# Beginning of a four-stage kernel: tokens loaded in two transfers, the second half's and the context's turns moved among the steps of the first norm

## The chip, the cores and the metric

The kernel runs on one core of one Trainium2 chip. The metric is the device time of one execution in microseconds (us). The median of three runs of the kernel before is 998.36 us (997.34 to 1002.92).

## The reference, cut to what matters

The program runs 1024 tokens (4 batches of 256) of width 256 through eight sublayers, each of the form `x = x + f(layernorm(x))`: expert FFN by token id, ternary FFN, WKV scan, mixture of experts, quantised attention, quantised FFN, linear attention, block-scaled FFN. The change touches only the first:

```
def _layernorm(x, axis=-1, eps=1e-05):
    m = jnp.mean(x, axis=axis, keepdims=True)
    v = jnp.var(x, axis=axis, keepdims=True)
    return (x - m) / jnp.sqrt(v + eps)
x = x + _L0_xattn_ref(_layernorm(x, axis=-1), itok_BxS_13_99985, ctx_2048, ctx_2048, ctx_2048)
...
for e in range(E):      # the expert's three weights are slices of ctx_2048
    g = jax.nn.silu(jnp.einsum('bsd,fd->bsf', hidden_states, Wg[e]))
    u = jnp.einsum('bsd,fd->bsf', hidden_states, Wu[e])
    y = jnp.einsum('bsf,df->bsd', g * u, Wd[e])
    out = jnp.where((expert_ids == e)[..., None], y, out)
```

So before the first product the kernel needs the tokens and the context with the feature dimension on the partitions, and the norm of the tokens.

## The kernel before, in words

Every engine has its own instruction list, written out by hand and executed in order; semaphores join them. The activations live transposed: `x_t` is 128 partitions x 2 feature blocks (KC) x 1024 tokens, and most work goes by halves of 512 tokens (TH = 2, HALF = 512). Half 0 is batches 0 and 1, half 1 is batches 2 and 3. The context is transposed likewise into `ctx_t`.

Loading. SyncE (SP) issues all DMAs of the beginning on one queue: tokens into `x_nat` (L648, semaphore load["x"]), context into `ctx_nat` (L649, load["ctx"]), token ids broadcast to all partitions (L650), and then the weights of several stages (helper `rows_in`, L656 and L658). Each DMA adds 16 to its semaphore when it has landed.

Turning. TensorE (PE) transposes 128x128 blocks with `pe.transpose` (L475, helper `pe_turn`). `tokens_turned` makes four groups for each of the two tensors, in the order (half 0, block 0), (half 0, block 1), (half 1, block 0), (half 1, block 1). So x has groups 0 to 3 and ctx groups 4 to 7. A group is four turns into one PSUM bank, 6 or 7 in alternation, and a copy out of it: even groups by ScalarE (ACT, L489), odd ones by VectorE (DVE, L487). A group may start when the group two before it has been copied out. `part_of(name, (i, n))` picks part i of n of the groups of a name; `evacuated` makes PE wait for a name's last two copies.

The norm "l0x" of half 0 is a chain over three engines: mean (`ln_mean_of`: four matmuls with `mean_w`, PE), centring (`ln_xc_of`, L2070, DVE), squares (`ln_sq_of`, L1667, ACT), sums of squares (`ln_var_of`: 16 matmuls with one column each, PE), square root (`ln_sd_of`, L1672, ACT, with another activation table), reciprocal and diagonal matrix (`ln_diag_of`, L2076 and L2080, DVE), rows (`ln_rows_of`: two matmuls, PE), product (`ln_xn_of`, L2086, DVE). The helper line of all these matmuls is L962. The mean waits for `x_ready`, which DVE raises after the copies. Half 1's norm is computed inside the expert stage, which follows as `ffn(l0x)`; DVE first makes the masks of the token ids for it (L2240 to L2244) and then gates (L2248, L2249). ACT's function there is Silu (L1702), in a third table.

In the kernel before, PE turns all of x, then computes the mean, turns all of ctx, and then does the sums and the rows.

Of the kernel before, what the change touches and what calls it, by code (L numbers as in the profile page):

```python
# [14 lines left out]
ACT = mybir.ActivationFunctionType  # L15
# [9 lines left out]
P = 128  # L25
D = 256
KC = D // P
BATCH = 4
SEQ = 256
TOK = BATCH * SEQ  # L30
TT = TOK // P
# [32 lines left out]
def build(nc, a, out, stop=None):  # L64
# [5 lines left out]
    with ExitStack() as ctx:  # L70
        def sb(name, shape, dt=F32):
            return ctx.enter_context(nc.sbuf_tensor(name, shape, dt))

        def sem(name):
            return ctx.enter_context(nc.semaphore(name))
# [3 lines left out]
        x_t = sb("x_t", [P, KC, TOK])  # L79
# [3 lines left out]
        sd = sb("sd", [P, TH, 4])  # L83
        rsd = sb("rsd", [P, TH, 4])
        rsd_diag = sb("rsd_diag", [P, 4, P])
        ctx_t = sb("ctx_t", [P, KC, TOK])
        act_buf = sb("act_buf", [P, 2, HALF])
        hid_buf = sb("hid_buf", [P, 2, HALF])
        ident = sb("ident", [P, P])
# [51 lines left out]
        c = Cut(0)  # L141
        ctx_nat = c([TT, D])
        x_nat = c([TT, D])
# [3 lines left out]
        c = Cut(c.at / 256)  # L147
# [6 lines left out]
        c = Cut(0)  # L154
# [4 lines left out]
        c = Cut(0)  # L159
# [4 lines left out]
        c = Cut(ARENA - 24 - 18)  # L164
# [5 lines left out]
        c = Cut(75.5)  # L170
# [26 lines left out]
        c = Cut(45.0625)  # L197

        slots = []
        for _ in range(2):  # L200
# [4 lines left out]
                d=c([KC, PACK + P]), dqa=c([PACK + P]), qb=c([P]), qb_rest=c([P]),  # L205
# [4 lines left out]
        def part_weights(b):  # L210
# [7 lines left out]
        c = Cut(0)  # L218
# [3 lines left out]
        c = Cut(0)  # L222
# [14 lines left out]
        c = Cut(0)  # L237
# [7 lines left out]
        c = Cut(92)  # L245
# [30 lines left out]
        c = Cut(0)  # L276
# [17 lines left out]
        c = Cut(c3.at / 256)  # L294
        wt_l3 = [c([KC, H3]), c([KC, H3]), c([8, D])]
        assert c.at / 256 <= late_at
        c = Cut(0)
# [13 lines left out]
        load = {n: sem("load_" + n) for n in ("ctx", "x", "tid", "l0", "l1", "mu", "moe0", "moe1",  # L311
                                               "l2w", "l2x", "l2", "l3x", "l3", "rows", "gate0", "gate1")}
        turned, evac_act, evac_dve = sem("turned"), sem("evac_act"), sem("evac_dve")
        weights_fixed = sem("weights_fixed")
        x_ready = sem("x_ready")
# [82 lines left out]
        def mark(name, f):  # L398
            first = len(groups)
            f()  # L400
            marks[name] = (first, len(groups))
# [12 lines left out]
        def tokens_turned(nat, dst, wait):  # L414
            for h in range(TH):
                for k in range(KC):
                    turns = [(P, P, j * P, nat[:, 4 * h + j, k * P:(k + 1) * P]) for j in range(4)]
                    groups.append((turns, [(dst[:, k, h * HALF:(h + 1) * HALF].unsqueeze(1), P, 0, 512, 512)],
                                   wait, 0))

        mark("x", lambda: tokens_turned(x_nat, x_t, (load["x"], 16)))
        mark("ctx", lambda: tokens_turned(ctx_nat, ctx_t, (load["ctx"], 16)))

        def three(ws, wts, h, wait, fixed):
            turn_in(h, ws[0], wts[0], wait, fixed)
# [39 lines left out]
        def pe_turn(pe, name, part=None):  # L465
            for g in part_of(name, part):
                turns, _, wait, fixed = groups[g]
                if g >= 2:
                    pe.wait_ge(*copied(g - 2))
                if wait:  # L470
                    pe.wait_ge(*wait)
                if fixed:
                    pe.wait_ge(weights_fixed, fixed)
                for m, w, col, src in turns:
                    last = pe.transpose(ps[0:m, 6 + g % 2, col:col + w], src, ident[0:src.shape[0], 0:src.shape[0]])  # L475
                last.then_inc(turned, 1)

        def copy_out(eng, name, dve, part=None):
            for g in part_of(name, part):
                if by_dve[g] != dve:  # L480
                    continue
                eng.wait_ge(turned, g + 1)
                for dst, m, col, step, n in groups[g][1]:
                    k = dst.shape[1]
                    src = ps[0:m, 6 + g % 2, col:col + k * step].rearrange("p (k n) -> p k n", k=k)[:, :, 0:n]
                    if dve:
                        last = eng.tensor_copy(dst, src)  # L487
                    else:
                        last = eng.activation(dst, src, ACT.Copy)  # L489
                last.then_inc(evac_dve if dve else evac_act, 1)  # L490
# [9 lines left out]
        def ffn_lag(s):  # L500
# [3 lines left out]
        l0x = dict(name="l0x", n=4 * KC, rows=[P] * 4 * KC,  # L504
                   w1=lambda k, i: ctx_t[:, k, i * P:(i + 1) * P], w3=None,
                   w2=lambda i, o: ctx_t[:, i % KC, (i // KC) * SEQ + o * P:(i // KC) * SEQ + (o + 1) * P])
# [138 lines left out]

        @block.sync
        def _(sp):
            sp.dma_start(x_nat, a["x"].rearrange("b (c p) d -> p (b c) d", p=P)).then_inc(load["x"], 16)  # L648
            sp.dma_start(ctx_nat, a["ctx_2048"].rearrange("b (c p) d -> p (b c) d", p=P)).then_inc(load["ctx"], 16)  # L649
            sp.dma_start(tid, a["itok_BxS_13_99985"].rearrange("b s -> (b s)").partition_broadcast(P)  # L650
                         ).then_inc(load["tid"], 16)
# [308 lines left out]
        def _(pe):  # L960
# [18 lines left out]
            def ln_var_of(name, h):  # L979

                n = 2 * LN[name] + h
                pe.wait_ge(ln_sq, n + 1)
                if n:

                    pe.wait_ge(xn_ready, n)
                for j in range(4):
                    for k in range(KC):
                        last = mm(ps[:, ln_row_bank(name, h), j:j + 1],
                                  ln_sq_tile(name, h)[:, k, j * P:(j + 1) * P], mean_w[:, 0:1],
                                  k == 0, k == KC - 1)  # L990
                last.then_inc(ln_var, 1)

            def ln_rows_of(name, h):

                pe.wait_ge(ln_diag, 2 * LN[name] + h + 1)
                mm(ps[:, ln_row_bank(name, h), :], ones[:, :], rsd_diag[:, :, :].rearrange("p a b -> p (a b)"), True,
                   True).then_inc(ln_rows, 1)
# [73 lines left out]
                return go  # L1071

            pe.wait_ge(const_ready, 1)
            pe_turn(pe, "x")
            ln_mean_of("l0x", 0)
            pe_turn(pe, "ctx")
            ln_var_of("l0x", 0)
            ln_rows_of("l0x", 0)
            evacuated(pe, marks["ctx"][1])

# [579 lines left out]
        def _(act):  # L1660
# [8 lines left out]
            def ln_sd_of(name, h):  # L1669
                n = 2 * LN[name] + h  # L1670
                act.wait_ge(ln_var, n + 1)
                act.activation(sd[:, h, :], ps[:, ln_row_bank(name, h), 0:4], ACT.Sqrt, bias=eps_col[:, :]  # L1672
                               ).then_inc(ln_sd, 1)
# [41 lines left out]
                    hidden_high(s, TH - 1, s["n"] - 1)  # L1715

            act.wait_ge(const_ready, 1)
            copy_out(act, "x", False)
            ln_sq_of("l0x", 0)
            copy_out(act, "ctx", False)  # L1720
            ln_sd_of("l0x", 0)
            def ternary_copied(name, wts, h, i):

                full, src, dst = h // P, ternary_back[name][i], wts[i]
                act.wait_ge(load[name], 16 * 8)
                if i == 2:
                    act.activation(dst.rearrange("p c (k j) -> p c k j", j=P),
                                   src.rearrange("p (k c j) -> p c k j", k=KC, j=P), ACT.Copy).then_inc(weights_fixed, 1)
                else:
                    v = src.rearrange("p (r k j) -> p k r j", k=KC, j=P)  # L1730
                    act.activation(dst[:, :, 0:full * P].rearrange("p k (r j) -> p k r j", j=P), v[:, :, 0:full], ACT.Copy)
                    act.activation(dst[:, :, full * P:], v[:, :, full, 0:h % P], ACT.Copy)
# [319 lines left out]
        def _(dve):  # L2052
# [14 lines left out]
            def ln_xc_of(name, h):  # L2067
                dve.wait_ge(ln_mean, 2 * LN[name] + h + 1)
                b = ln_bank(name, h)
                TTN(xc[:, h], x_t[:, :, tok(h)], ps[:, b:b + 1, :].to_broadcast([P, KC, HALF]), ALU.subtract  # L2070
                    ).then_inc(ln_xc, 1)

            def ln_diag_of(name, h):
                n = 2 * LN[name] + h
                dve.wait_ge(ln_sd, n + 1)
                step(dve.reciprocal(rsd[:, h, :], sd[:, h, :]))  # L2076
                if n:

                    dve.wait_ge(ln_rows, n)
                TTN(rsd_diag[:, :, :], ident[:, :].unsqueeze(1).to_broadcast([P, 4, P]),  # L2080
                    rsd[:, h, :].unsqueeze(2).to_broadcast([P, 4, P]), ALU.mult).then_inc(ln_diag, 1)

            def ln_xn_of(name, h):
                dve.wait_ge(ln_rows, 2 * LN[name] + h + 1)
                b = ln_row_bank(name, h)
                TTN(xn_t[:, :, tok(h)], xc[:, h], ps[:, b:b + 1, :].to_broadcast([P, KC, HALF]), ALU.mult  # L2086
                    ).then_inc(xn_ready, 1)
# [138 lines left out]
                step(last)  # L2226
                return TTN(v, v, b3(scale, MX_BLOCK), ALU.mult)

            copy_out(dve, "x", True)
            dve.wait_ge(evac_act, 2)  # L2230
            dve.wait_ge(evac_dve, 2)
            dve.sem_inc(x_ready, 2)
            ln_xc_of("l0x", 0)
            copy_out(dve, "ctx", True)
            ln_diag_of("l0x", 0)
            ln_xn_of("l0x", 0)

            dve.wait_ge(load["tid"], 16)
# [606 lines left out]
```

## Time and profile before

| | |
|---|---|
| median of three runs | 998.36 us (997.34, 998.36, 1002.92) |
| profiled execution, time | 1001.22 us |
| its span | 999.5 us |
| its mean granted TensorE clock | 0.91 of full |
| PE busy | 854.2 us, 85% of the span |
| DVE / ACT / POOL busy | 716.6 / 452.1 / 164.8 us |
| chain that ended last | PE 54%, DVE 26%, ACT 9% |

The profile is one execution; its engines are PE (matmul), PEld (weight load of the same engine, overlapping), DVE, ACT, POOL and SP's DMA queue. The span begins with the first instruction, and all times are microseconds from there. The time of the execution is 1.7 us longer than its span.

### The profile page before, as it was taken

Reading aid. Unit: us, or ns where it says so; the run is one execution under the profiler, and the core shown is the slowest. Engines: PE = TensorE matmul, PEld = TensorE weight load, DVE = VectorE, ACT = ScalarE, POOL = GpSimd, SP = SyncE. Lnnn points to the kernel's source line nnn. Section 1 sums busy time; section 2 is a strip of 40 time slices with the busy share of each in tenths; the row PEclk is TensorE's granted clock in tenths of the full one; section 3 lists DMA queues with packets and bytes.
Section 4 is the critical chain, followed back from the end, with each engine's and each line's share of the span. In section 5 each row is a group of like instructions: output and inputs, shape, how many; then the busy total and the mean of one; then the engine's idle time right before and its main releaser. Section 6 shows DMA issues by size and latency. Waiting matters only on the chain.

```text
span 999.5 us, 12145 instructions
## 1 busy us (share of the span) xinstructions
PE 854.2 (85%) x4470; PEld 521.9 (52%) x4470; DVE 716.6 (72%) x962; ACT 452.1 (45%) x695; POOL 164.8 (16%) x251
## 2 busy tenths in 40 slices
PE   5989984489889999999899787777778989889898
PEld 3434652244645555555455444445454758755566
DVE  1676669964557888778669889899894544459677
ACT  2214546642334322222123489899894545522111
POOL 1000000000004523334400063111110000002312
PEclk9899995579979999999999979898799999879899
DMA  8602003100132222141021899998781000000000
GB/s 256 216 0 48 1 0 57 13 3 7 17 51 41 36 29 34 44 66 17 3 45 31 156 172 168 165 164 141 143 136 39 21 0 1 1 1 1 10 11 22
DMA packets 211614, 59.17 MB, mean 59 GB/s; under 512 B 192398, under 2 KB 209892, under 8 KB 211556
## 3 DMA queue, kind: packets, MB, share of 16 engines
q1 hardware_dynamic: 211508, 58.30, 30.4%
q8 instruction: 36, 0.59, 0.2%
q10 hardware_dynamic: 48, 0.10, 0.1%
q14 instruction: 22, 0.18, 0.1%
HBM read 20.62 MB, written 1.05 MB: 22 GB/s over the span
## 4 chain that ended last, share of the span: by engine, by line
PE 54%; DVE 26%; ACT 9%; issue 8%; DMA 1%; POOL 1%; SPq 0%; DVEq 0%; ACTq 0%; POOLq 0%
PE ps L962 50%; ACT xc L1935 2%; DVE arena L2651 2%; PE ps L1412 1%; ACT sq L1935 1%; DVE arena L2285 1%; PE ps L475 1%; DVE arena L2660 1%; DVE arena L2215 1%; DVE xc L2457 1%; PE ps L1093 1%; DVE sq L2564 1%; ACT arena_split L1850 1%; DVE sq L2561 1%; DVE xc L2070 1%
## 5 line engine op out<-in xcount | busy, mean ns | idle before, releaser
L962 PE MATMUL ps<-arena 128*128 128x16 f16 (+8 forms) x1776 | 248.9, 296 | 47.3 <-ACT xc L1935 22.4
L962 PE MATMUL ps<-arena_split 128*128 128x512 f32 (+6 forms) x736 | 195.9, 429 | 17.2 <-DVE arena_split L2107 5.9
L962 PEld LDWEIGHTS ps<-arena 128*128 128x128 f16 (+4 forms) x1776 | 136.1, 125 | 122.3 <-issue 67.0
L962 PEld LDWEIGHTS ps<-arena_split 128*128 128x128 f32 (+6 forms) x736 | 131.7, 192 | 88.1 <-issue 39.7
L2651 DVE TENSOR_REDUCE arena<-ps 128x1 f32<-128x1024 f32 x128 | 151.5, 1220 | 14.8 <-PE ps L962 13.6
L1935 ACT ACTIVATE xc<-ps,arena 128x1024 int16<-128x1024 f32 x86 | 103.0, 1208 | 12.0 <-POOL arena L919 11.5
L962 PE MATMUL ps<-sq,arena 128*64 128x256 f32 (+3 forms) x256 | 78.7, 504 | 8.1 <-DVE sq L2564 8.0
L868 POOL TENSOR_SCALAR arena<-arena 128x512 f32<-128x512 f32 x12 | 23.1, 1922 | 245.3 <-DVE arena L2479 245.3
L919 POOL TENSOR_SCALAR arena<-arena 128x1 f32<-128x1 f32 x128 | 33.9, 265 | 177.5 <-DVE arena L2651 177.2
L1702 ACT ACTIVATE act_buf<-ps 128x512 f32<-128x512 f32 (+2 forms) x34 | 20.3, 596 | 85.5 <-PE ps L962 85.4
L1935 ACT ACTIVATE sq<-ps,arena 128x1024 int16<-128x1024 f32 x42 | 50.4, 1210 | 3.7 <-POOL arena L919 3.5
L962 PEld LDWEIGHTS ps<-sq,arena 128*64 128x64 f32 (+3 forms) x256 | 29.2, 161 | 42.2 <-issue 29.8
L962 PE MATMUL ps<-arena,ident_b 128*128 128x256 bf16 x224 | 49.3, 307 | 0.0
L962 PE MATMUL ps<-mean_w,sq 128*128 128x1 f32 x240 | 32.9, 267 | 18.5 <-ACT sq L1667 18.5
L936 POOL TENSOR_TENSOR arena<-arena 128x1024 f32<-128x1024 f32 (+1 forms) x9 | 17.5, 1948 | 184.2 <-DVE arena L2223 184.1
L962 PEld LDWEIGHTS ps<-mean_w,sq 128*128 128x128 f32 x240 | 32.7, 216 | 26.7 <-ACT sq L1667 24.7
L962 PE MATMUL ps<-x_t,mean_w 128*128 128x512 f32 x64 | 37.9, 723 | 7.9 <-DVE x_t L2307 4.4
L962 PE MATMUL ps<-xn_t,arena 128*128 128x256 f32 (+2 forms) x112 | 38.4, 489 | 0.0
L1850 ACT ACTIVATE arena_split<-xc 128x1024 fp32r<-128x1024 f32 x16 | 16.9, 1059 | 40.3 <-DVE xc L2457 40.3
L475 PE MATMUL ps<-ident,arena 128*128 128x128 f32 (+4 forms) x122 | 22.8, 342 | 14.1 <-DMA arena<-in_x 7.1
L2395 DVE TENSOR_TENSOR hid_buf<-ps,act_buf 128x512 f32<-128x512 f32 (+2 forms) x18 | 12.4, 690 | 30.5 <-ACT act_buf L1702 30.2
L962 PE MATMUL ps<-xn_t,ctx_t 128*128 128x512 f32 x64 | 33.0, 645 | 1.4 <-DVE xn_t L2086 1.4
(300 smaller groups left out, 1342.6 us busy)
## 6 DMA issues: line engine op xcount, KB each, us to landing
arena<-in_L_ffn_w SPq DMA_DIRECT2D x4, 640.0 KB, 6.1
arena_split<-arena_split SPq DMA_DIRECT2D x61, 32.0 KB
arena<-in_x SPq DMA_DIRECT2D x1, 1024.0 KB, 6.2
arena<-in_ctx SPq DMA_DIRECT2D x1, 1024.0 KB, 8.6
arena<-in_L_xattn_Wkv SPq DMA_DIRECT2D x2, 512.0 KB, 4.0
arena<-in_L_ffn_gate_w SPq DMA_DIRECT2D x1, 1024.0 KB, 10.1
arena<-in_L_ffn_up_w SPq DMA_DIRECT2D x1, 1024.0 KB, 12.6
arena<-in_L_ffn_down_w SPq DMA_DIRECT2D x1, 1024.0 KB, 12.6
```

What stands on the lines that cost most here:

```text
L475: last = pe.transpose(ps[0:m, 6 + g % 2, col:col + w], src, ident[0:src.shape[0], 0:src.shape[0]])
L868: step(pool.tensor_scalar(qf, qf, 2.0 ** -6, 1.5 * 2.0 ** 20, ALU.max, ALU.mult))
L919: pool.tensor_scalar(A["bias"][:, b:b + 1], A["nm"][:, b:b + 1], A["sq"][:, t, i:i + 1], math.log(255.0), ALU.mult, ALU.add).then_inc(att_ ...
L936: return pool.tensor_tensor(v, v, scale.unsqueeze(2).to_broadcast([P, n, MX_BLOCK]), ALU.mult)
L962: return pe.matmul(o, l, r, start=start, stop=stop)
L1093: return pe.transpose(ps[0:m, bank, col:col + n], src, ident[0:n, 0:n])
L1412: last = pe.transpose(ps[:, 7, :].bitcast(BF16)[:, k * P:(k + 1) * P], y[:, k * P:(k + 1) * P], ident_b[:, :])
L1702: act.activation(act_buf[0:r, u % 2, :], ps[0:r, 2 * (u % 2), :], func, scale=1.0 if scale is None else scale[0:r, :]).then_inc(act_ready, 1)
L1850: act.activation(moe["xe_parts"][:, n % 2, 0], moe["xe"], ACT.Copy).then_inc(moe_xh, 1)
L1935: act.activation(probs(u).rearrange("p (a b) -> p a b", a=2), ps[:, score_banks(u), :], ACT.Exp, bias=att_small["bias"][:, u % 3:u % 3 + 1 ...
L2395: return TTN(hid, up, s, ALU.mult)
L2651: dve.tensor_reduce(A["nm"][:, b:b + 1], ps[:, score_banks(u), :], AX.XY, ALU.max, negate=True).then_inc(att_max, 1)
```

## The change

The tokens come in two transfers of half the size; the second adds to load["ctx"], so that the value 32 means that the second half and the context are there, and 16 on load["x"] that the first half is. PE turns the first half, computes its mean, turns the second half and the first half of the context, does the sums, turns the context's second half, and does the rows. ACT and DVE place their copies accordingly. DVE raises `x_ready` once for each half. ACT begins with a copy of 128x4 elements into `sd`, which is overwritten later.

```
--- before.py
+++ after.py
@@ -416,10 +416,10 @@
                 for k in range(KC):
                     turns = [(P, P, j * P, nat[:, 4 * h + j, k * P:(k + 1) * P]) for j in range(4)]
                     groups.append((turns, [(dst[:, k, h * HALF:(h + 1) * HALF].unsqueeze(1), P, 0, 512, 512)],
-                                   wait, 0))
-
-        mark("x", lambda: tokens_turned(x_nat, x_t, (load["x"], 16)))
-        mark("ctx", lambda: tokens_turned(ctx_nat, ctx_t, (load["ctx"], 16)))
+                                   wait[h], 0))
+
+        mark("x", lambda: tokens_turned(x_nat, x_t, ((load["x"], 16), (load["ctx"], 32))))
+        mark("ctx", lambda: tokens_turned(ctx_nat, ctx_t, ((load["ctx"], 32), (load["ctx"], 32))))
 
         def three(ws, wts, h, wait, fixed):
             turn_in(h, ws[0], wts[0], wait, fixed)
@@ -645,7 +645,10 @@
 
         @block.sync
         def _(sp):
-            sp.dma_start(x_nat, a["x"].rearrange("b (c p) d -> p (b c) d", p=P)).then_inc(load["x"], 16)
+            sp.dma_start(x_nat[:, 0:TT // 2, :], a["x"][0:BATCH // 2].rearrange("b (c p) d -> p (b c) d", p=P)
+                         ).then_inc(load["x"], 16)
+            sp.dma_start(x_nat[:, TT // 2:TT, :], a["x"][BATCH // 2:BATCH].rearrange("b (c p) d -> p (b c) d", p=P)
+                         ).then_inc(load["ctx"], 16)
             sp.dma_start(ctx_nat, a["ctx_2048"].rearrange("b (c p) d -> p (b c) d", p=P)).then_inc(load["ctx"], 16)
             sp.dma_start(tid, a["itok_BxS_13_99985"].rearrange("b s -> (b s)").partition_broadcast(P)
                          ).then_inc(load["tid"], 16)
@@ -1071,10 +1074,12 @@
                 return go
 
             pe.wait_ge(const_ready, 1)
-            pe_turn(pe, "x")
+            pe_turn(pe, "x", (0, 2))
             ln_mean_of("l0x", 0)
-            pe_turn(pe, "ctx")
+            pe_turn(pe, "x", (1, 2))
+            pe_turn(pe, "ctx", (0, 2))
             ln_var_of("l0x", 0)
+            pe_turn(pe, "ctx", (1, 2))
             ln_rows_of("l0x", 0)
             evacuated(pe, marks["ctx"][1])
 
@@ -1715,10 +1720,12 @@
                     hidden_high(s, TH - 1, s["n"] - 1)
 
             act.wait_ge(const_ready, 1)
+            act.activation(sd[:, 0, :], ident[:, 0:TT // 2], ACT.Copy)
             copy_out(act, "x", False)
             ln_sq_of("l0x", 0)
-            copy_out(act, "ctx", False)
+            copy_out(act, "ctx", False, (0, 2))
             ln_sd_of("l0x", 0)
+            copy_out(act, "ctx", False, (1, 2))
             def ternary_copied(name, wts, h, i):
 
                 full, src, dst = h // P, ternary_back[name][i], wts[i]
@@ -2226,13 +2233,18 @@
                 step(last)
                 return TTN(v, v, b3(scale, MX_BLOCK), ALU.mult)
 
-            copy_out(dve, "x", True)
+            copy_out(dve, "x", True, (0, 2))
+            dve.wait_ge(evac_act, 1)
+            dve.wait_ge(evac_dve, 1)
+            dve.sem_inc(x_ready, 1)
+            ln_xc_of("l0x", 0)
+            copy_out(dve, "x", True, (1, 2))
             dve.wait_ge(evac_act, 2)
             dve.wait_ge(evac_dve, 2)
-            dve.sem_inc(x_ready, 2)
-            ln_xc_of("l0x", 0)
-            copy_out(dve, "ctx", True)
+            dve.sem_inc(x_ready, 1)
+            copy_out(dve, "ctx", True, (0, 2))
             ln_diag_of("l0x", 0)
+            copy_out(dve, "ctx", True, (1, 2))
             ln_xn_of("l0x", 0)
 
             dve.wait_ge(load["tid"], 16)
```

## Rows read from the trace of the kernel before

**Rows 1.** The page: granted clock in 40 slices (tenths); chain by engine

```profile
PEclk9899995579979999999999979898799999879899
...
PE 54%; DVE 26%; ACT 9%; issue 8%; DMA 1%; POOL 1%; SPq 0%; DVEq 0%; ACTq 0%; POOLq 0%
```

**Rows 2.** Chain of waits, 0 to 35 us: start, duration, what

```profile
0.81 6.18 DMA arena<-in_x
...
7.12 1.10 PE ps L475 x4
...
8.29 1.28 ACT L489
...
16.85 1.23 DVE xc L2070
```

**Rows 3.** DMA issues and rates: size, time to landing; SP's issues; stretches with GB/s last

```profile
arena<-in_x SPq DMA_DIRECT2D x1, 1024.0 KB, 6.2
arena<-in_ctx SPq DMA_DIRECT2D x1, 1024.0 KB, 8.6
...
arena<-in_L_xattn_Wkv SPq DMA_DIRECT2D x1, 512.0 KB, 4.0
...
arena<-in_L_ffn_down_w SPq DMA_DIRECT2D x1, 1024.0 KB, 12.6
...
1.33 0.56 SPq L649 DMA_DIRECT2D arena<-in_ctx  x1
...
28.39 4.13 SPq L656 DMA_DIRECT2D arena<-in_L_ffn_down_w  x1
...
1.80:3.40 1.60, 0.00 (x0) 0.00 (x0) 0.00 (x0) 0.00 (x0) 1.17 (x4) 1.00 0.78 156
3.40:5.40 2.00, 0.00 (x0) 0.00 (x0) 0.00 (x0) 0.00 (x0) 1.13 (x4) 1.00 0.97 330
5.40:7.00 1.60, 0.00 (x0) 0.00 (x0) 0.00 (x0) 0.00 (x0) 0.00 (x0) 1.00 1.09 371
```

**Rows 4.** Timeline of PE, 0 to 34 us: start, duration, work, count, idle before

```profile
13.04 3.78 PE L962 MATMUL ps<-x_t,mean_w 128*128 128x512 f32 x4 [0.83 <-DVEq L2232]
16.61 1.91 PE L475 MATMUL ps<-ident,arena 128*128 128x128 f32 x8
19.70 1.10 PE L475 MATMUL ps<-ident,arena 128*128 128x128 f32 x8 [1.18 <-ACT ctx_t L489]
20.64 1.84 PE L962 MATMUL ps<-mean_w,sq 128*128 128x1 f32 x16
23.77 2.08 PE L962 MATMUL ps<-rsd_diag,ones 128*128 128x512 f32 x2 [1.29 <-DVE rsd_diag L2080]
```

**Rows 5.** PE at the other level, and granted clock (third from the end) by stretch

```profile
35.26 1.88 PE L962 MATMUL ps<-x_t,mean_w 128*128 128x512 f32 x4
...
52.50 1.02 PE L962 MATMUL ps<-rsd_diag,ones 128*128 128x512 f32 x2
...
164.04 3.58 PE L962 MATMUL ps<-mean_w,sq 128*128 128x1 f32 x16 [5.84 <-ACT sq L1667]
...
24.00:30.00 6.00, 4.59 (x6) 1.50 (x7) 3.98 (x6) 0.08 (x1) 0.00 (x0) 0.50 1.09 338
```

**Rows 6.** Timeline of ACT, 0 to 34 us and around 870 us

```profile
31.04 0.60 ACT L1702 ACTIVATE act_buf<-ps 128x512 f32<-128x512 f32 x1 [6.96 <-PE ps L962]
...
868.60 0.26 ACT L1672 ACTIVATE sd<-ps,eps_col 128x4 f32<-128x4 f32 x1
871.44 0.60 ACT L489 ACTIVATE arena<-ps 128x512 f32<-128x512 f32 x1 [2.58 <-PE ps L475]
```

**Rows 7.** Timeline of DVE, 0 to 34 us and around 102 us

```profile
27.02 2.14 DVE L2240 TENSOR_SCALAR arena<-arena 128x1024 bf16<-128x1024 int32 x3
...
31.75 0.69 DVE L2248 TENSOR_TENSOR hid_buf<-ps,act_buf 128x512 f32<-128x512 f32 x1 [0.21 <-ACT act_buf L1702]
...
101.90 0.68 DVE L2259 TENSOR_REDUCE arena<-arena 128x16 f32<-128x512 f32 x1
```

## The prediction, made before the result was known

> **What bounds the kernel now.** I read the page first: PE holds 54% of the chain that ended last, DVE 26% [rows 1], so far from the beginning a microsecond saved on another engine is worth nothing. Then the chain of waits from 0 to 35 us, because the change is only there: it holds the transfer of the tokens until 6.99, turns from 7.12, a table load of 1.28 at 8.29 and the centring at 16.85 [rows 2]; between them, on PE, mean, turns, sums and rows, each behind an idle gap or behind another's copy [rows 4]. PE is a bystander in much of it; what is cut from this chain moves everything behind it. Third, the timelines of PE, ACT and DVE for durations [rows 4, 6, 7], the DMA issues and rates [rows 3], and rows of the same work elsewhere at both clock levels [rows 5]. Nothing later waits for a transfer of the beginning: the last big weight load is issued at 28.39 and the like take 12.6 us to land, so about 41, and its first reader, a DVE reduction, starts at 101.90 [rows 3, 7]. So I carry a gain at the norm to the end one for one.
>
> **Clock.** The granted-clock column reads 1.00 up to 22, but durations say otherwise: four mean matmuls took 3.78 us at 13.04 and four of the same 1.88 at 35.26; eight turns took 1.91 at 16.61 and 1.10 at 19.70 [rows 4, 5]. So PE worked at 1.2 GHz until about 19.2, at 2.4 for the turns and the sums of squares, and at 1.2 again for the rows (2.08 at 23.77, 1.02 at 52.50) and the start of the expert stage (0.50 in the column from 24 to 30) [rows 4, 5]. The rise came some 6 us after PE began its unbroken stretch at 13.04.
>
> **The change step by step** (new times are estimates in the profile's own scale).
> 1. Tokens in two transfers. Now issue at 0.81, landing 6.18 later, first turn at 7.12 [rows 2, 3, 4]. From the rates, 156, 330 and 371 GB/s in the three stretches [rows 3], the first 0.52 MB have moved by 1.8 + 1.6 + 0.83 = 4.2 us and the full 1.05 MB by 5.8: 1.5 us less to wait. The other bound is a 512 KB transfer alone, 4.0 us instead of 6.2: 2.2 less. On the unfavourable side, 0, if the two halves interleave. I take 1.7, nearer to the same queue at the same moment: first turn at 5.42. SP issues one more DMA, 0.56 us at most, like its neighbour [rows 3]; context is issued at about 1.8 instead of 1.33. It lands now at 9.9 (1.33 + 8.6), so at 9.9 (same bytes ahead of it) to 10.5. Token ids and weights are queued behind it and are late by as much at most; DVE asks for the ids only behind the norm, at 27.02 [rows 7].
> 2. Table load. ACT loads a table for 1.28 us after the first turns, at 8.29, and PE's second eight turns wait for the copy behind it [rows 2]. The added 128x4 copy takes the load ahead of the landing, with ACT idle. It costs nothing: ACT has nothing else before 6.5.
> 3. First half. Eight turns 1.94, DVE copy 0.69 and signals 0.1: the mean starts 2.75 after the first turn, at 8.17. Before it started at 13.04, so 4.87 earlier: 1.7 from the transfer, 3.17 from turns, table load and copies of the second half that no longer stand ahead of it [rows 2, 4]. The 0.69 of a copy is the length of DVE's 128x512 piece at 31.75 [rows 7]. The centring follows at 3.81, as before (13.04 to 16.85): 11.98 to 13.20 [rows 2].
> 4. Second half behind the mean. The mean's matmuls let the next turn begin 3.57 later (13.04 to 16.61), at 11.74, later than context's 10.5, so the joint wait for second half and context is covered by the mean; the cover is 1.2 to 1.8 us wide. Eight turns at low clock, 1.91: to 13.65. ACT copies their first half 12.8 to 13.4 and squares after it, 13.4 to 14.46 (1.06), about 0.2 later than centring alone would allow. DVE copies the second half 13.68 to 14.37 (0.69) [rows 4, 6, 7].
> 5. Context's first half. Its first four turns can start at 13.45 and its other four only after DVE's copy, at 14.42. Four turns take 0.47 at high clock (eight in 0.94, from 19.70 to the sums at 20.64) and about 0.9 at low. Everything behind them on PE waits: the sums of squares. If the clock rises as long after the mean's start as before, it does so at about 14.4, and the sums start at 14.9, with bounds 14.46 (high from the start; then the end of the squares decides) and 15.3 (low). Before: 20.64. Gain 5.8, with bounds 5.3 and 6.2 [rows 4].
> 6. Sums of squares, 1.84 at high clock like before; the low-clock row is 3.58, bound 1.7 worse [rows 4, 5].
> 7. Context's second half goes into PE's idle 1.29 us between sums and rows [rows 4], where ACT does sd, DVE reciprocal and diagonal. Eight turns take 1.10 at high clock: hidden. At low, 1.94: rows 0.65 late. Queued behind: on ACT a copy of 0.6 after sd; on DVE a copy of 0.69 after the diagonal, under the rows (2.08). A copy after a square root needs no table load: at 871.44 ACT does just that [rows 6]. ACT's load of the next table (1.28) comes after that copy; ACT was idle 6.96 us before its first Silu at 31.04 [rows 6], which covers both.
> 8. Rows: 2.08 as before; if the clock holds, 1.02, a bound of 1.06 better [rows 4, 5]. Norm and the start of the expert stage follow unchanged.
> 9. The expert stage. From norm to the first down projection PE isn't alone: DVE makes masks from 27.02 on and gates at 31.75, only 0.21 after its last idle [rows 7]. A higher clock there gains little before the first product with the gated values. Taken as 0.
>
> **Sum.** 1.7 (transfer) + 3.2 (second half off the path) + context's turns and their two waits, which stood between the centring and the sums (16.85 to 20.64 = 3.79, now 11.98 to 14.9 = 2.9), 0.9 = 5.8 us. The profiled execution took 1001.22 (span 999.5), so 995.4 in its own terms. It stands 2.9 above the median of the runs shown, 998.36; from that, 992.6.
>
> The Trainium skill speaks against the split: "DMA: Bandwidth & Descriptors", section Bandwidth, wants transfers batched to at least 1 MiB. Its fit of about 2.0 us fixed plus bytes over 436 GB/s (for another issuing path) makes the first wait 3.2 instead of 4.4, 1.2 us less where I take 1.7; by it the sum would be 5.3. The trace pays 6.2 for 1 MB and 4.0 for 512 KB [rows 3], a larger difference.
>
> **Rivals.**
> A. The clock is low in the sums. For: it is free to move, and the profile shows both prices. Against: PE works here 5.4 us unbroken before, and the like sufficed at 19.7. Cost 1.7 + 0.65 + 0.4: gain 3.0, 995.3. Chance 0.17.
> B. The halves don't land one after the other, or the context's landing slips past 11.7 and the joint wait decides. For: both halves and context share the DMA engines, which are full from 3.4 on [rows 3]. Against: 1 MB landed at 7.0 though context was issued 0.5 behind it. Gain 5.8 - 1.7 = 4.1: 994.3. Chance 0.08.
> C. The high level comes already with the second half's turns and holds through the rows: 5.8 + 0.4 + 1.06 = 7.3, 991.1. Chance 0.10.
> D. Slower. The chain moves, but the clock's low stretches later fall elsewhere. The place is the PE-bound rest [rows 1]: each microsecond of low clock in dense work costs half a microsecond, as the pairs of prices show (3.78 and 1.88) [rows 4, 5]. It decides from 12 us of additional low clock on; 22 us give 992.6 + 11 = 1003.6. For: the three runs before spread over 5.6 us, and the page's clock row has dips throughout [rows 1]. Against: low stretches fall as often better as worse. Chance 0.06.
>
> **From cases to numbers.** Forecast 0.59, for gains of 4.5 to 7. What a measurement can tell from no change is 0.5%, 5.0 us, so 993.4. Of the forecast 0.49 lies beyond it and 0.10 short of it, as the transfer's 1.7 and the sums' start are uncertain by about 1 us. Faster: 0.49 + C 0.10 = 0.59. Within 0.5%: 0.10 + A 0.17 + B 0.08 = 0.35. Slower: D 0.06. The likeliest gives 992.6; its own range is 991.4 to 993.9. The range reaches C with some clock luck (989.0) and A with some bad luck (996.6); it leaves out D and the outer parts of A and C, under 2 in 10.
>
> **What would show it.** First turn at about 5.4 (step 1); ACT's table load before 4 (2); mean at 8.2 (3); no idle time on PE between mean and second half's turns (4); squares at 13.4, sums at 14.5 to 15.3 (5), lasting 1.8 and not 3.6 (6); rows 1.3 to 2.0 after the sums (7); norm at about 20.1 instead of 25.89. Wrong, if context lands after 11.7, if a table load shows up between sd and copy, or if the stretch from the norm on is longer than before by as much as the beginning is shorter.

## The result, and the profile after

| | before | after |
|---|---|---|
| median of 14 timings, us | 1000.21 (996.25 to 1004.65) | 991.91 (986.90 to 998.24) |
| profiled execution: time, span, mean clock | 1001.22, 999.5, 0.91 | 996.42, 994.0, 0.914 |

The ratio is 0.9909, 95% interval 0.9886 to 0.9931: 9.1 us less, between 6.9 and 11.4. The forecast was 992.6, 5.8 less; direction and time hold, but 5.8 lies below the interval: the gain was sized too small. The 14 timings of the kernel before hold the three known before the forecast, with median 998.36; the other eleven have median 1000.66. Ratios, here and below, leave out the executions that took over 1.5% longer than their kernel's fastest; medians and counts keep them.

PE's timeline of the changed kernel, 0 to 28 us (start, duration, work, count, idle before):

```profile
4.98 1.94 PE L475 MATMUL ps<-ident,arena 128*128 128x128 f32 x8 [4.98 <-POOLq L856]
7.75 3.78 PE L965 MATMUL ps<-x_t,mean_w 128*128 128x512 f32 x4 [0.83 <-DVEq L2239]
11.32 3.35 PE L475 MATMUL ps<-ident,arena 128*128 128x128 f32 x16
14.51 1.84 PE L965 MATMUL ps<-mean_w,sq 128*128 128x1 f32 x16
16.21 1.07 PE L475 MATMUL ps<-ident,arena 128*128 128x128 f32 x8
17.64 1.12 PE L965 MATMUL ps<-rsd_diag,ones 128*128 128x512 f32 x2 [0.36 <-DVE rsd_diag L2087]
20.18 5.37 PE L965 MATMUL ps<-xn_t,ctx_t 128*128 128x512 f32 x8 [1.41 <-DVE xn_t L2093]
25.97 1.98 PE L965 MATMUL ps<-hid_buf,ctx_t 128*128 128x512 f32 x4 [0.43 <-DVE hid_buf L2261]
```

Against [rows 2, 4]: the first turn is 2.14 us earlier (7.12 to 4.98), the mean 5.29 (13.04 to 7.75), the sums of squares 6.13 (20.64 to 14.51), the rows 6.13 (23.77 to 17.64). From the mean to the sums the timeline shows no idle gap of PE any more. The eight turns of the context's second half lie in the place of the idle 1.29. The rows last 1.12 instead of 2.08.

ACT's and DVE's timelines of the same execution:

```profile
0.80 1.28 ACT L1723 ACT_TABLE_LOAD   x1 [0.80 <-PEq L2847]
...
6.10 0.60 ACT L489 ACTIVATE x_t<-ps 128x512 f32<-128x512 f32 x1 [3.67 <-PE ps L475]
...
12.91 1.05 ACT L1672 ACTIVATE sq<-xc 128x1024 f32<-128x1024 f32 x1
...
16.39 0.26 ACT L1677 ACTIVATE sd<-ps,eps_col 128x4 f32<-128x4 f32 x1 [0.53 <-PE ps L965]
16.88 0.60 ACT L489 ACTIVATE ctx_t<-ps 128x512 f32<-128x512 f32 x1 [0.23 <-PE ps L475]
17.50 1.28 ACT L1707 ACT_TABLE_LOAD   x1
```

```profile
6.96 0.69 DVE L487 COPY x_t<-ps 128x512 f32<-128x512 f32 x1 [6.96 <-PE ps L475]
11.56 1.22 DVE L2077 TENSOR_TENSOR xc<-x_t,ps 128x1024 f32<-128x1024 f32 x1 [3.92 <-PE ps L965]
...
18.81 1.22 DVE L2093 TENSOR_TENSOR xn_t<-xc,ps 128x1024 f32<-128x1024 f32 x1 [0.62 <-PE ps L965]
...
91.13 1.22 DVE L2099 TENSOR_TENSOR x_t<-ps,x_t 128x1024 f32<-128x1024 f32 x1 [0.94 <-PE ps L965]
```

The table load has gone to 0.80, and none stands between the square root at 16.39 and the copy at 16.88. The norm product starts at 18.81 instead of 25.89: 7.08 earlier. The last line is DVE's final addition of the first expert stage. In the kernel before these two lines read:

```profile
25.89 1.22 DVE L2086 TENSOR_TENSOR xn_t<-xc,ps 128x1024 f32<-128x1024 f32 x1 [2.17 <-PE ps L962]
...
98.60 1.22 DVE L2092 TENSOR_TENSOR x_t<-ps,x_t 128x1024 f32<-128x1024 f32 x1 [0.94 <-PE ps L962]
```

So 7.47 us are gained by then. I use this line below as the mark of the stage's end. After it the two executions run the same work; at the end of the spans the distance is 5.5. That the low clock, falling at other places, moved it is the likeliest reason, but is not shown for this pair.

One name in these lines misleads. The page puts PE's first wait down to POOL (L856), whose last signal of the constants came at about the same moment. PE asks for the first signal only, and in three executions below, in which PE began at 4.88, 4.90 and 4.92, the page names the transfer.

### The profile page after: what moved, and what is told of

Same layout as the page of the kernel before. It is cut to its first block, busy times and chain, and to the rows that moved or that the text cites. A ratio compares the mean times of both kernels' runs of the same rounds, so it can differ in the third digit from the quotient of the medians.

```text
span 994.0 us, 12147 instructions
## 1 busy us (share of the span) xinstructions
PE 853.5 (86%) x4470; PEld 521.9 (53%) x4470; DVE 715.9 (72%) x962; ACT 451.9 (45%) x696; POOL 164.7 (17%) x251
## 3 DMA queue, kind: packets, MB, share of 16 engines
HBM read 20.62 MB, written 1.05 MB: 22 GB/s over the span
## 4 chain that ended last, share of the span: by engine, by line
PE 54%; DVE 27%; ACT 10%; issue 8%; POOL 1%; SPq 0%; DMA 0%; DVEq 0%; ACTq 0%; POOLq 0%
PE ps L965 49%; ACT xc L1942 2%; DVE arena L2663 2%; ACT sq L1942 1%; PE ps L1417 1%; DVE arena L2297 1%; PE ps L475 1%; DVE arena L2222 1%; PE ps L1098 1%; DVE xc L2469 1%; DVE arena L2672 1%; ACT arena_split L1857 1%; DVE sq L2576 1%; DVE sq L2573 1%; DVE arena L2206 1%
## 5 line engine op out<-in xcount | busy, mean ns | idle before, releaser
L965 PE MATMUL ps<-arena 128*128 128x16 f16 (+8 forms) x1776 | 245.9, 293 | 47.3 <-ACT xc L1942 22.4
L965 PE MATMUL ps<-sq,arena 128*64 128x256 f32 (+3 forms) x256 | 80.9, 514 | 8.0 <-DVE sq L2576 8.0
L1848 ACT ACTIVATE act_buf<-ps 128x512 f32<-128x512 f32 x16 | 9.6, 598 | 56.2 <-PE ps L965 56.2
L2475 DVE TENSOR_TENSOR arena_split<-xc,arena_split 128x1024 fp32r<-128x1024 f32 x16 | 21.1, 1316 | 18.0 <-ACT arena_split L1857 18.0
```

The source lines that it names most:

```text
L965: return pe.matmul(o, l, r, start=start, stop=stop)
L2475: TTN(parts[:, n % 2, 1], moe["xe"], parts[:, n % 2, 0], ALU.subtract).then_inc(moe_xl, 1)
```

## The experiments

Single timings of one kernel scatter by 2 to 5 us (standard deviation), so the profile's marks are read beside the medians. Each mark comes from one execution. Together, 34 timings of the changed kernel have mean 992.6 and 93 of the kernel before 1001.2: 8.6 less, plus or minus 1.5 (the 93 are those taken beside the experiments, without the 14 of the table; with them it is 8.5).

**The changed kernel again**, beside the next three (`a_again`), and once more beside the last three (`a_third`). No edit.

> The changed kernel once more, as the measure for its neighbours on this chip. Theory (the beginning is 7.1 us shorter at the norm and passes that on one for one): 7 us less than before, norm product at 18.8. Rival (something outside the beginning also got quicker, since 14 runs gave 8.3 less): 9 us or more with the norm product still at 18.8.

> The changed kernel a third time, beside these three on their chip. Theory: 7 to 9.5 us below the kernel before. Rival: under 7 or over 9.5, that is, the difference depends on the chip.

Measured: 991.68, ratio 0.9905 (0.9865 to 0.9945); and 994.23, ratio 0.9934 (0.9904 to 0.9963). Stage's end at 91.12 and 92.53. In the third execution the clock was low for the rows (2.08), and the norm product came at 19.67. By the ratios the differences are 9.5 and 6.6. Each is what its rival wanted (9 or more; under 7), one on either side of the theory. But the two intervals share the stretch from 0.9904 to 0.9945, so neither something outside the beginning nor a difference between chips is shown by them. The held-back kernel below bears on the first.

**The tokens in one transfer** (`a_one_transfer`):

```
-sp.dma_start(x_nat[:, 0:TT // 2, :], ...).then_inc(load["x"], 16)
-sp.dma_start(x_nat[:, TT // 2:TT, :], ...).then_inc(load["ctx"], 16)
+sp.dma_start(x_nat, a["x"]...).then_inc(load["x"], 16)
```

The second half's turns wait for load["x"] as well.

> The changed kernel with the tokens in one transfer again; the second half's turns wait for the same transfer. Theory (the split is worth what the first half lands earlier, 2.1 us, since everything behind the first turn hangs on it): first turn at 7.1, norm product 2.1 later, at 20.9, time 2.1 above the changed kernel. Rival (the clock's rise is tied to when PE begins work and swallows or doubles it): norm product 1.0 or 3.5 later.

Measured: 994.46, ratio 0.9924 (0.9895 to 0.9954). Its DMA issue, its turns, and what came of them:

```profile
arena<-in_x SPq DMA_DIRECT2D x1, 1024.0 KB, 5.6
```

```profile
6.50 1.94 PE L475 MATMUL ps<-ident,arena 128*128 128x128 f32 x8 [6.50 <-DMA arena<-in_x]
9.27 3.78 PE L962 MATMUL ps<-x_t,mean_w 128*128 128x512 f32 x4 [0.83 <-DVEq L2236]
12.85 1.28 PE L475 MATMUL ps<-ident,arena 128*128 128x128 f32 x8
```

One megabyte landed in 5.6 us here, not in 6.2, so the first turn was 1.5 later, not 2.1; the norm product came at 19.86, 1.05 later. Half a microsecond went back because the second half's turns (12.85) were mostly at the high clock: eight in 1.28, where the changed kernel took 1.91. That is the rival's number, but only half for its reason: 0.6 of the missing 1.1 is a quicker landing, 0.5 the clock.

At the stage's end the distance is no longer 1.05 but 2.71 (91.12 in the run beside it):

```profile
21.22 3.67 PE L962 MATMUL ps<-xn_t,ctx_t 128*128 128x512 f32 x8 [1.40 <-DVE xn_t L2090]
27.02 3.64 PE L962 MATMUL ps<-hid_buf,ctx_t 128*128 128x512 f32 x4 [2.12 <-DVE hid_buf L2258]
...
93.83 1.22 DVE L2096 TENSOR_TENSOR x_t<-ps,x_t 128x1024 f32<-128x1024 f32 x1 [0.94 <-PE ps L962]
```

The additional 1.7 is the price of the first down projections at the low clock, 3.64 where the changed kernel took 1.98; more on that under the held-back kernel. In the medians the difference to the run beside it is 2.8. That fits the mark, but is within the scatter.

**Without the early table load** (`a_no_preload`):

```
-act.activation(sd[:, 0, :], ident[:, 0:TT // 2], ACT.Copy)
```

> The changed kernel without the early 128x4 copy, so that the table load of 1.28 us stands ahead of the first copy. Theory A (my prediction's step: it stands on the path): mean and norm product 1.3 later. Theory B (the mean waits for two copies, and DVE's, which ends at 7.66, covers most of it: ACT's would end at 6.1 + 1.3 + 0.6 = 8.0): norm product 0.35 later, 19.2, and nothing that the time can show.

Measured: 992.18, ratio 0.9911 (0.9875 to 0.9948), against 0.9905 beside it. The lines of ACT and PE:

```profile
6.09 1.28 ACT L489 ACT_TABLE_LOAD   x1 [6.09 <-PE ps L475]
7.39 0.60 ACT L489 ACTIVATE x_t<-ps 128x512 f32<-128x512 f32 x1
```

```profile
8.12 3.78 PE L965 MATMUL ps<-x_t,mean_w 128*128 128x512 f32 x4 [1.26 <-DVEq L2238]
...
14.89 1.84 PE L965 MATMUL ps<-mean_w,sq 128*128 128x1 f32 x16
...
18.02 2.08 PE L965 MATMUL ps<-rsd_diag,ones 128*128 128x512 f32 x2
```

Theory B: mean and sums are 0.37 and 0.38 later (8.12 against 7.75). In the new order the load hides behind DVE's copy for all but that. The norm product came at 20.14, because the rows fell to the low clock. They can do so with the early load in place: the third execution of the changed kernel had the same, and against it (19.67) the norm product is 0.47 later. The stage's end is at 94.14, 3.0 later than at 91.12 beside it. 1.7 of that is again the low clock in the first down projections (3.67), and nothing of it is clear in the time.

**The context turned in one piece ahead of the sums** (`a_ctx_together`):

```
 pe_turn(pe, "x", (1, 2))
-pe_turn(pe, "ctx", (0, 2))
+pe_turn(pe, "ctx")
 ln_var_of("l0x", 0)
-pe_turn(pe, "ctx", (1, 2))
```

and the copies of ACT and DVE likewise.

> The changed kernel with the context turned in one piece ahead of the sums of squares. Theory (moving the second half into the gap behind the sums took its turns and one wait for a copy off the path): sums 1.4 later, at 15.9, norm product 1.4 later, 20.2. Rival (the turns in the gap are what keeps the clock high for the rows): then the rows take 2.1 instead of 1.1 as well and the norm product comes 2.4 later, 21.2.

Measured: 995.18, ratio 0.9941 (0.9909 to 0.9973).

```profile
15.54 1.84 PE L965 MATMUL ps<-mean_w,sq 128*128 128x1 f32 x16
18.67 1.66 PE L965 MATMUL ps<-rsd_diag,ones 128*128 128x512 f32 x2 [1.29 <-DVE rsd_diag L2085]
```

Sums 1.03 later (15.54 against 14.51; the theory said 1.4), norm product at 20.37, 1.56 later: 1.03 for the turns and the copies that they wait for, 0.54 for rows that straddle a fall of the clock. Full low-clock rows as the rival wanted didn't come. But this one execution doesn't refute it: with the turns in the gap the rows took 1.12, 1.12 and 2.08 in three executions of the changed kernel, so whether turns there keep the clock high stays open.

**One part alone on the kernel before.** `b_split`, the tokens in two transfers (the context's landing is counted on the ids' semaphore, and the second half waits by itself); `b_preload`, the line of the early copy; `b_mean_first`:

```
-pe_turn(pe, "x")
+pe_turn(pe, "x", (0, 2))
 ln_mean_of("l0x", 0)
+pe_turn(pe, "x", (1, 2))
```

with DVE's copies and `x_ready` by halves.

> The kernel before with the tokens in two transfers and nothing else; the context's landing is counted on the token ids' semaphore so that the second half can be waited for by itself. Theory (each half is turned as it lands; the second lands about 1.4 us behind the first and PE's copies take longer than that): first turn at 4.9, mean at 13.0 - 2.1 = 10.9, norm product 2.1 earlier, 23.8, unless the clock's rise moves. Rival (a split alone gains nothing because the mean needs both halves there): mean at 12.5 or later.

> The kernel before with the early 128x4 copy and nothing else. Theory (what covers the table load in the changed kernel, the mean behind DVE's copy, isn't there before: the second half's turns wait for the copy behind the load): mean 1.3 earlier, at 11.8, norm product 24.6. Rival (covered here too): mean unchanged at 13.0.

> The kernel before with the mean and the centring ahead of the second half's turns, in one transfer, without the early copy and with the context turned in one piece. Theory (order alone): mean at 7.12 + 2.75 + 0.35 = 10.2, so 2.8 earlier; eight turns then stand between mean and context's turns, sums about 1.5 earlier than before, norm product 24.4. Rival (an earlier unbroken stretch on PE brings the clock up earlier too): norm product 23 or earlier.

Measured: b_split 999.65, ratio 0.9997 (0.9975 to 1.0018); b_preload 1000.27, 0.9982 (0.9954 to 1.0010); b_mean_first 998.17, 0.9986 (0.9964 to 1.0008). None is clear of no change. PE's timeline of b_split:

```profile
5.07 1.94 PE L475 MATMUL ps<-ident,arena 128*128 128x128 f32 x8 [5.07 <-POOLq L856]
...
10.98 3.78 PE L965 MATMUL ps<-x_t,mean_w 128*128 128x512 f32 x4 [0.83 <-DVEq L2235]
...
18.58 3.07 PE L965 MATMUL ps<-mean_w,sq 128*128 128x1 f32 x16
22.94 2.08 PE L965 MATMUL ps<-rsd_diag,ones 128*128 128x512 f32 x2 [1.29 <-DVE rsd_diag L2083]
```

Mean 2.06 earlier, as the theory has it, and sums 2.06 earlier. Then the sums take 3.07 instead of 1.84, as the clock falls within them, and rows and norm product (25.06) are only 0.83 earlier. In b_preload the mean is at 11.43, 4.67 behind its first turn instead of 5.92: 1.25 gained, so the load stood on the path before in full. Its sums took 3.09 as well, and the norm product, at 25.52, is 0.37 earlier, which is no more than its quicker landing (first turn at 6.76). In b_mean_first the norm product is at 22.36 instead of 25.89. Its first turn, at 6.50, was 0.6 early by luck of the landing, and the clock rose within the mean (3.56). Order alone thus brings about 2.9 of its 3.5, what the earlier rise of the clock gave included; that is the rival's outcome and not the theory's 1.5. The three parts alone give 2.1 (first turn and mean), 1.25 (mean) and 2.9 (norm product) at the marks where each acts. Of the 2.1 only 0.83 is left at the norm product, and of the 1.25 nothing, the quicker landing taken off. At the stage's end the three stand 0.55, 0.11 and 3.93 before the kernel before. The changed kernel, which also moves the context's second half into the gap (1.0 of the sums in a_ctx_together), has 7.08 at the norm product and 7.47 at the stage's end.

**The changed kernel held back** (`a_delay`):

```
 step(pool.tensor_copy(ident_b[:, :], ident[:, :]))
+for _ in range(38):
+    step(pool.memset(act_buf[:, 0, 0:P], 0.0))
```

> The changed kernel, held back: GpSimd clears 128 columns of an unused buffer 38 times before it releases the identity, so that the first turn starts at about 12.2 instead of 4.98 and the rest of the beginning follows in the changed order. Theory (the whole gain is the 7.25 us by which the first down projection comes earlier, passed on one for one): first down projection at about 33.2 and the time of the kernel before, within 2 us. Rival (the new order brings more than the profile of the beginning shows, because ten timings put the gain at 8 to 9): still 2 us or more below the kernel before.

Measured: 1000.88, ratio 1.0004 (0.9974 to 1.0034).

```profile
12.24 1.97 PE L475 MATMUL ps<-ident,arena 128*128 128x128 f32 x8 [12.24 <-POOLq L841]
...
27.03 3.67 PE L967 MATMUL ps<-xn_t,ctx_t 128*128 128x512 f32 x8 [1.41 <-DVE xn_t L2095]
32.82 3.54 PE L967 MATMUL ps<-hid_buf,ctx_t 128*128 128x512 f32 x4 [2.12 <-DVE hid_buf L2263]
```

The kernel before has, for the same work:

```profile
27.25 6.46 PE L962 MATMUL ps<-xn_t,ctx_t 128*128 128x512 f32 x8 [1.41 <-DVE xn_t L2086]
33.55 1.88 PE L962 MATMUL ps<-hid_buf,ctx_t 128*128 128x512 f32 x4
```

The norm product came at 25.66 and the first down projection at 32.82, 0.23 and 0.73 earlier than before. With the first turn held back by 7.26, the time is that of the kernel before, within an interval from 2.6 below it to 3.4 above. So the gain lies in the beginning, as the theory has it. How exactly a microsecond there is one at the end can't be told to better than some 3 us: a rest of 2 below, with which the rival began, is just inside the interval. No sign of it shows, though, for the stage's end is 1.08 later than in the kernel before, and not earlier:

```profile
99.68 1.22 DVE L2101 TENSOR_TENSOR x_t<-ps,x_t 128x1024 f32<-128x1024 f32 x1 [0.94 <-PE ps L967]
```

The last two lines of a_delay's PE timeline above show why. Here the first products ran at the high clock, eight in 3.67; PE then stood still for 2.12, and the four down projections behind it ran at the low clock, 3.54 instead of 1.98 in the changed kernel. From the norm product to the down projection it still took 7.16, as in the changed kernel (18.81 to 25.97), where the products took 5.37. Sorted by the eight first products, the twelve executions with the masks in place show three lengths of the stretch from norm product to stage's end:

| first products | idle of PE behind them | four down projections | down projection behind norm product | norm product to stage's end | executions |
|---|---|---|---|---|---|
| 5.1 to 5.8 (the clock rises within them) | 0.2 to 0.7 | 1.98 | 7.2 to 7.3 | 72.3 to 72.5 | 5 (the changed kernel's first two, a_ctx_together, b_mean_first, a_warm) |
| 6.5 to 6.7 (low nearly throughout) | none | 1.88 | 7.7 to 7.9 | 72.7 to 73.0 | 4 (the kernel before, the changed kernel's third, b_split, b_preload) |
| 3.67 (high throughout) | 2.12 | 3.54 to 3.67 (low nearly throughout) | 7.16 | 74.0 | 3 (a_one_transfer, a_no_preload, a_delay) |

So the place of the low clock alone moves the end of this stage by up to 1.7 us.

**The masks later** (`a_masks_later`):

```
-for e in range(1, 4):
-    step(TS(ge_mask[:, e - 1, :], tid, ...))
+at_least(1)          # at_least(2), at_least(3) and three further masks after gates 0 to 4
```

> The changed kernel with only the first token mask (two operations, 1.1 us) ahead of the first gate and the other five operations after gates 0 to 4. Theory (between norm product and first down projection two chains run side by side, DVE's masks and PE's first products at the low clock with ACT's Silu, and are equally long): first down projection earlier by 0.1 to 1.8, the more the higher the clock, time 0 to 2 lower. Rival (the deferred masks push the gates behind them): expert stage 1 us longer, time not lower.

Measured: 993.41, ratio 0.9938 (0.9911 to 0.9965), beside the changed kernel's 0.9934. Norm product (19.44) to first down projection (24.98): 5.54 instead of 7.16, so the masks were the bound there. The first products ran at the high clock (3.67), but PE idled 0.50 behind them instead of 2.12, and the down projections stayed at the high clock (1.98). Stage's end 90.21 instead of 91.13, though the norm product was 0.6 later in this execution. The timings don't show it.

**Turns of the identity to occupy PE** (`a_warm`), and both together with eight more ahead of the first product (`a_warm_masks`):

```
 pe.wait_ge(const_ready, 1)
+for _ in range(11):
+    pe.transpose(ps[:, 0, 0:P], ident[:, :], ident[:, :])
 pe_turn(pe, "x", (0, 2))
+for _ in range(3):
+    pe.transpose(ps[:, 0, 0:P], ident[:, :], ident[:, :])
```

> The changed kernel with 11 turns of the identity into a free bank while PE waits for the first half, and 3 while it waits for the copies ahead of the mean; their results are not used. Theory (PE does the mean and the second half's turns at the low clock only because it was idle before; work ahead of them raises the clock before the mean ends): mean 2 to 3.8 us long instead of 3.8, norm product 1 to 2 us earlier, 17 to 17.8, time 1 to 2 below the changed kernel. Rival (such turns don't raise the clock, or it falls again before the rows): norm product at 18.8 or later, up to 20.

> The two together: turns of the identity ahead of the first half and the mean, eight more while PE waits for the norm product, and the masks later. Theory: norm product at 16.8 as with the warm turns alone, first products at the high clock, first down projection about 5.0 after it (20.6 + 1.5 = at 22) instead of 7.2: 4 us earlier than in the changed kernel (25.97), time 3 to 4 below it. Rival (the clock falls all the same before the first products, as it did at 20.4): first down projection at 23.5 to 24, time 2 below.

Measured: a_warm 992.51, ratio 0.9899 (0.9862 to 0.9937), where three measurements of the changed kernel, none of them beside it, gave 0.9909, 0.9905 and 0.9934; a_warm_masks 992.23, ratio 0.9924 (0.9896 to 0.9952), measured beside the latter. PE in a_warm:

```profile
2.26 2.61 PE L1078 MATMUL ps<-ident 128*128 128x128 f32 x11 [2.26 <-POOLq L839]
...
7.69 2.28 PE L965 MATMUL ps<-x_t,mean_w 128*128 128x512 f32 x4 [0.18 <-DVEq L2243]
...
12.38 1.94 PE L965 MATMUL ps<-mean_w,sq 128*128 128x1 f32 x16
...
15.61 1.12 PE L965 MATMUL ps<-rsd_diag,ones 128*128 128x512 f32 x2 [0.36 <-DVE rsd_diag L2091]
```

The mechanism works: the mean takes 2.28 instead of 3.78, the sums come at 12.38 instead of 14.51, the norm product at 16.77 instead of 18.81, and the stage ends at 89.08 instead of 91.13. With the masks later it ends at 88.34. That is 2.0 and 2.8 us in the profile, and nothing of it is clear in the time. For the two together the theory wanted the norm product at 16.8, the first down projection at 22 and a time 3 to 4 below the changed kernel's. They came at 17.64 and 23.11, because the clock was low for the turns in the gap and the rows (1.90 and 1.92), and the median is 2.0 below: the theory missed, and in the time it is the rival's 2. Nothing here shows a loss behind the stage, but 9 and 12 timings with this scatter can't show 2 us. So no version beats the changed kernel by what was measured.

## Why the prediction was right, and where it was too small

**Direction and mechanism.** Steps 2 to 7 happened in their order. The mean came 2.77 behind the first turn (said 2.75), the next turn 3.57 behind the mean, with no wait for the joint landing; the squares ran from 12.91 to 13.96 (said 13.4 to 14.46); no table load came up between square root and copy. "One for one" (that a gain at the norm reaches the end) is borne out by a_delay within about 3 us.

**Step 1, the transfer.** I took 1.7 between 1.5 and 2.2; the first turn came 2.14 earlier. The 512 KB transfer alone, 4.0 us [rows 3], was the better row. But the kernel before was itself profiled with a slow landing, 6.2, where one megabyte took 5.6 and 5.8 in three other executions; against those (first turns at 6.50 and 6.76) the split is worth about 1.5 to 1.8. So it is one profiled execution that makes the term look short by 0.4.

**Step 2.** I gave the early load its place, and the sum gave it and the second half's move 3.2 together. The runs divide it: moving the second half covers the load for all but 0.38, while in the old order taking it early is worth 1.25 at the mean. Costed each for itself they would have been counted twice; the sum was safe because it was taken as the distance from first turn to mean.

**Step 5.** Sums said at 14.9, came at 14.51: the 0.4 of the transfer. The clock's rise, taken at 14.4, came among the context's turns, between 13.0 and 14.5.

**Step 8, the rows.** This is the term that was mis-sized: 2.08 taken, 1.12 measured, 0.96 of the 1.3 us that the norm product came before the forecast (20.1 against 18.81). I had it as a bound and as rival C. The clock was still high at 17.64, with PE busy in the gap behind the sums where before it had idled. But in the third execution of the same kernel the rows took 2.08; it isn't the order alone that decides. In two of the three executions the gain at the norm was thus nearer to rival C's 7.3, which had 0.10, than to the forecast's 5.8, which had 0.59.

**Step 9, the expert stage taken as 0.** The reason given holds in part: a higher clock than the changed kernel's in the first products brings the down projection no earlier (7.16 behind the norm product in a_delay too). But the 0 isn't right. The stage's end gained 0.39 more than the norm product (7.47 against 7.08), as norm product to down projection took 7.66 in the kernel before, with its products at the low clock for longer. And products wholly at the high clock, with the idle time behind them, cost 1.7 in the down projections. That price was missing from the sum; rival D has its like, but places it in the PE-bound rest.

**The base.** Norm product plus stage make 7.5 us; the ratio gives 9.1 with 7.5 inside its interval. But the one profiled execution of the kernel before had the slow landing; against a landing of 5.6 or 5.8 the same marks would give 6.9 to 7.1, an estimate. The three timings known lay 1.9 under the median of all fourteen, so "998.36 less 5.8" met the measured time with two errors that cancel: gain too small by 2.5 (the medians differ by 8.3), base too low by 1.9. That the time came within 0.7 is luck in that sense; direction and mechanism aren't. Rival D's mechanism is real, and goes with most of the scatter: 0.01 more of mean granted clock goes with 4 us less time (a line through the 233 timings that the ratios use, with a level of its own for each kernel and each repeat; scatter around it 2.0 us). At equal clock the changed kernel's first 14 timings stand 7.7 (plus or minus 1.1) below the kernel before, those of a_again 7.3 (1.4) and of a_third 6.0 (1.3), all together 7.0 (0.8). The marks of the stage's end in the same three say 7.5, 7.5 and 6.1. The mean granted clock of these timings was 0.917 for the changed kernel and 0.913 for the one before, which by the line makes up the rest of the 8.6; why it was higher isn't shown. Rival A (sums at the low clock) didn't happen in the changed kernel's three executions, but did in part where one edit stood alone (3.07 and 3.09). Rival B: the context's landing didn't decide in these three: the turns that wait for it began 3.57 behind the mean, with no idle time.

## What to carry to other kernels

At a kernel's beginning, let the first transfer hold only what the first link of the chain needs, and put the rest of the loading's work behind the waits of that chain: each piece alone may be too small to measure, and the sum isn't. Cost such edits as distances between marks (first turn, mean, sums, product), because what one edit removes another may already cover. And where a clock scatters the times by 3 us, take the profile's marks for the mechanism, several executions' marks where they depend on a landing or on the clock, and many timings for the base. Read a mark behind the place of the change too: here a stretch of low clock made 1.05 us at the norm product into 2.71 at the stage's end.

## What the runs showed of the hardware that I had not expected

The same megabyte of tokens landed after 6.2, 5.8, 5.6 and 5.6 us in four executions of kernels with one transfer.

PE work whose result nobody reads counts for the clock: with 2.61 us of turns of a constant matrix ahead of the first half and 0.84 ahead of the mean, the high clock came within the mean (2.28 instead of 3.78, a_warm). Without them, in every execution of the changed kernel and of those made from it, it came behind the mean. In the changed kernel's first execution it came among the context's first turns, for the second half's eight still took 1.91; in others, a_masks_later for one (1.57), it was among the second half's turns, though PE had done the same work up to there.

The first eight products at the high clock and then 2.12 us of idle PE were followed by four down projections at the low clock, 3.54 to 3.67 us, in all three executions that had this (a_delay, a_one_transfer, a_no_preload). With the same products and 0.50 us of idle time they took 1.98 (a_masks_later, a_warm_masks).
